# Two factor transfers swapped on ScalarE's queue, two merge groups regrouped by batch, and six fewer products of zeros, at the start of a conditioned mixture-of-experts kernel

## The reference, cut to what matters

```
def cond(x, ids, wi, wo, common, experts):      # first block, once per batch
    hidden = x @ wi.T + 2 * (x @ cia.T) @ cib.T + 2 * (x @ Eia[id].T) @ Eib[id].T
    hidden = relu(hidden)
    return hidden @ wo.T + 2 * (hidden @ coa.T) @ cob.T + 2 * (hidden @ Eoa[id].T) @ Eob[id].T
...
for r in range(4):                              # mixture of experts, on the result
    w = top-2 softmax of cur @ Wg[r] + bg[r]
    cur = cur + sum_e w_e * (gelu(cur @ W1[e] + b1[e]) @ W2[e] + b2[e])
x = x + cur
...                                             # second block: language factors, ternary net
```

## Time and profile before

| what | value |
|---|---|
| time before, median of 3 runs | 481.5 us (481.15 to 481.94) |
| the profiled execution's own time | 481.59 us |
| its span, first to last instruction | 479.9 us |
| TensorE busy | 475.6 us, 99% of the span |
| VectorE, ScalarE, GpSimd busy | 388.1, 393.7, 121.4 us |

### The profile page before, as it was taken

One profiled execution on the slowest core, in us unless ns is written; L12 is line 12 of the kernel. 1 busy time (PEld: TensorE's weight loads), 2 busy tenths in 40 slices (PEclk: granted clock), 3 DMA queues, 4 the chain that ended last, 5 costly groups with the idle time before them and its releaser, 6 DMA issues.

```text
span 479.9 us, 7453 instructions
## 1 busy us (share of the span) xinstructions
PE 475.6 (99%) x2268; PEld 396.2 (83%) x2268; DVE 388.1 (81%) x638; ACT 393.7 (82%) x543; POOL 121.4 (25%) x102
## 2 busy tenths in 40 slices
PE   9999999999999999999999999999999999999997
PEld 8998888888888888888888888888888888888886
DVE  4899899999989898988898898889897758654343
ACT  4889888888888898888888788898888888697644
POOL 3995212121211212121212121271313144500000
PEclk9999999999999999999999999999999999999999
DMA  7504702020120202020202012120202000000001
GB/s 237 188 24 133 286 1 89 2 88 13 77 82 6 88 0 88 0 88 0 88 1 87 23 65 84 48 89 0 88 2 88 2 0 0 1 1 0 0 23 69
DMA packets 8299, 27.03 MB, mean 56 GB/s; under 512 B 2258, under 2 KB 3602, under 8 KB 6098
## 3 DMA queue, kind: packets, MB, share of 16 engines
q1 hardware_dynamic: 7090, 22.45, 13.1%
q0 software_dynamic: 288, 2.88, 1.6%
q10 hardware_dynamic: 896, 1.38, 0.9%
HBM read 25.26 MB, written 1.44 MB: 56 GB/s over the span
## 4 chain that ended last, share of the span: by engine, by line
PE 97%; POOL 2%; DVE 0%; ACT 0%; issue 0%; DVEq 0%; POOLq 0%
PE bank L538 34%; PE bank L541 34%; PE bank L544 26%; POOL ffn_lo L442 1%; PE bank L634 1%; PE bank L638 1%; PE bank L639 1%; PE bank L565 1%; POOL xlo L447 0%; PE bank L562 0%; DVE stage L1076 0%; DVE prod L1076 0%; ACT ffn_hi L842 0%; DVE x L1312 0%; POOL blank L430 0%
## 5 line engine op out<-in xcount | busy, mean ns | idle before, releaser
L859 ACT ACTIVATE act_out<-bank,vec 128x512 f32<-128x512 f32 x256 | 165.0, 682 | 40.4 <-PE bank L544 28.2
L1154 DVE TENSOR_TENSOR hid_lo<-act_out,hid_hi 128x1024 fp32r<-128x1024 f32 x128 | 158.6, 1258 | 31.6 <-ACT hid_hi L864 31.5
L864 ACT ACTIVATE hid_hi<-act_out 128x1024 fp32r<-128x1024 f32 x128 | 135.9, 1062 | 8.2 <-ACT act_out L859 0.4
L502 POOL TENSOR_TENSOR cur<-cur,prod 128x512 f32<-128x512 f32 x48 | 64.9, 1352 | 233.6 <-DVE prod L1165 233.1
L538 PE MATMUL bank<-hid_hi,moe_hi 128*128 128x512 f32 x256 | 99.8, 390 | 0.0
L544 PE MATMUL bank<-hid_hi,moe_lo 128*128 128x512 f32 x256 | 99.7, 390 | 0.0
L541 PE MATMUL bank<-hid_lo,moe_hi 128*128 128x512 f32 x256 | 99.7, 389 | 0.0
L538 PE MATMUL bank<-xhi,moe_hi 128*128 128x512 f32 x256 | 99.6, 389 | 0.0
L541 PE MATMUL bank<-xlo,moe_hi 128*128 128x512 f32 x256 | 99.6, 389 | 0.0
L544 PE MATMUL bank<-xhi,moe_lo 128*128 128x512 f32 x256 | 99.6, 389 | 0.0
L538 PEld LDWEIGHTS bank<-hid_hi,moe_hi 128*128 128x128 f32 x256 | 48.1, 188 | 11.1
(11 more groups left out here) (134 smaller groups left out, 573.7 us busy)
## 6 DMA issues: line engine op xcount, KB each, us to landing
cw_all<-cw_dram SPq DMA_DIRECT2D x16, 1024.0 KB, 4.7
stage<-ffn_w POOLq DMA_DIRECT2D x1, 2304.0 KB, 8.5
cw_all<-moe_w SPq DMA_DIRECT2D x4, 512.0 KB, 6.9
stage<-lora_all SPq DMA_DIRECT2D x5, 160.0 KB, 3.8
x<-x_t SPq DMA_DIRECT2D x3, 256.0 KB, 4.2
out_t<-x SPq DMA_DIRECT2D x3, 256.0 KB, 2.5
cur<-cond_base ACTq DMA_DIRECT2D x2, 256.0 KB, 3.4
stage<-ffn_w POOLq DMA_DIRECT2D x1, 512.0 KB, 4.1
```

Source lines behind the costliest of these rows:

```text
L502: pool.tensor_tensor(cur[:, c, :], cur[:, c, :], prod[:, s % 2, :], ALU.add).then_inc(add_done, 1)
L859: act.activation(act_out[:, f // 2, f % 2, :], bank[:, f, :], ACT.Gelu_apprx_tanh, bias=vec[:, V_B1 + e * FC + f:V_B1 + e * FC + f + 1]).t ...
L864: act.activation(hid_hi[:, s % 2, 2 * pr:2 * pr + 2, :], act_out[:, pr, :, :], ACT.Copy)\
L1154: dve.tensor_tensor(hid_lo[:, s % 2, 2 * pr:2 * pr + 2, :], act_out[:, pr, :, :], hid_hi[:, s % 2, 2 * pr:2 * pr + 2, :].bitcast(F32), ALU ...
```

## The change

Three edits. In ScalarE's queue the second part of the base weights is issued ahead of the factors of batch 3 (the fourth batch). The third and fourth merge group, which held kind 0 and then kind 1 of batches 2 and 3, now hold both kinds of batch 2 and then both of batch 3, with banks 4 and 5 for batch 2 and 6 and 7 for batch 3. The products of zeros become ten (were 12) ahead of the first group and two (were 6) behind the second.

```
-                ((2, 0), (3, 0)),
-                ((2, 1), (3, 1)),
+                ((2, 0), (2, 1)),
+                ((3, 0), (3, 1)),
...
-MERGE_BANKS = (6, 7, 2, 3, 5, 4, 6, 7, 4, 6, 7, 4, 6, 7, 4, 6)
+MERGE_BANKS = (6, 7, 2, 3, 4, 5, 6, 7, 4, 6, 7, 4, 6, 7, 4, 6)
...
-WARM, KEEP_WARM = 12, 6
+WARM, KEEP_WARM = 10, 2
...
             first_load(act, 1)
+            base_load(act, 1)
             lora_load(act, 3)
-            base_load(act, 1)
```

## The result

The changed kernel takes 482.11 us (median of 22 executions, 481.50 to 485.75), the kernel before in the same session 481.51 us (22 executions, 480.52 to 482.24). The ratio is 1.0020, 95% interval 1.0011 to 1.0028. The forecast was 481.1 us, 0.4 us faster, in a range of 480.4 to 482.0. The changed kernel is slower by 0.6 us, just above the upper end of that range.

The account below looks back on a forecast made before the run. TensorE, busy 99%, bounds the kernel; only its start before 18.95 us can move. GpSimd's path gains 0.42 us and TensorE's 0.43, so 0.42 us off the 481.5 median gives 481.1 us, range 480.4 to 482.0.

Parts of the forecast that it names:

- What sets the time: Work from 18.95 us on moves as a block; the change is worth how much earlier that work starts.
- Ten leading products of zeros: TensorE's start: first group at 5.65 us, VectorE's first sum 0.42 us earlier, bounds 0 and 0.83 us.
- The third group: TensorE's merges: needs batch 2 alone, landing at 8.1 us, so it starts about 8.15 us.
- The swap: ScalarE's queue: batch 3's factors land at 8.5 us; second sum releases the fourth group at 8.85; swap alone worth nothing.
- late fourth batch: Fourth group: batch 3's factors queue behind 256 KB and slip; 481.4 to 481.5 us; chance 0.24 shared with similar cases.
- met even without the swap: VectorE's sum of (0, 1): second base part lands at 8.5 us, before the sum's start at 8.67.
- Regrouping at nothing: Third and fourth groups: strips run side by side, fourth takes at most 1.10 us; regrouping alone worth nothing.
- Two products of zeros behind the second group: TensorE free at about 8.1 us; removed 0.96 us is open on its side, other things then decide.
- The clock rival: TensorE at 1.2 GHz after pauses until about 14 us: 2.3 us lost, 483.4 us, +0.4%; chance 0.06.

Follow-up runs that it names:

- filled-in zeros: The changed kernel with four more products of zeros between the third and fourth merge group: 482.65 us against 481.33, ratio 1.0030.
- the old groups and a pause of 1.7 us: The kernel before with the swap and ten and two products of zeros, old merge groups kept: 482.15 us against 481.33, ratio 1.0022.
- zeros alone: The kernel before with ten and two products of zeros instead of twelve and six, transfers and groups as before: 480.90 us against 481.31, ratio 0.9993.

## Why the prediction was wrong

**What sets the time: right.** The work behind 19 us moved as a block (457.84 of 457.85 us busy after), and over the table the profiled time is 463.8 to 464.4 us more than the sixth group's start in all rows but that of eight leading zeros.

**Ten leading products of zeros: right in kind.** The first group starts at 5.66 us (forecast 5.65), set by the factors' landing. The first sum came 0.82 us earlier in the first trace and 0.23 in the second (7.66), around the forecast 0.42; but the kernel before has it at 7.46 in its second profile. TensorE's change of level comes at another time in each execution: the 24 passes of zeros took 5.49 us in one trace of the kernel before and 5.23 in the other. Alone, this edit measured 0.5 and 0.1 us faster, both within chance.

**The third group: right.** 7.97 us against 8.15, and 8.78 in the second trace, where batch 2's factors landed at 8.7.

**The swap: the step that failed.** The text took 8.5 us for the landing of batch 3's factors, "bounds 7.9 ... and 8.8", because ScalarE's two transfers together had landed by 8.5 before. They land at 9.1 to 9.5 us in the traces of five of the kernels above that have the swap, and at 8.8 only in the one with filled-in zeros. The sum of bytes on the queue did not hold: the transfer took 4.4 to 5.0 us from its issue where the bound allowed 4.2. Nor was the 3.3 us of the earlier trace rows firm: with the old order the same transfer takes 2.9 to 4.4 us in the ten traces and lands at 6.9 to 8.4, in the kernel's own second profile at 8.4. The fourth group was therefore released by a DMA at 9.54 and not by the second sum at 8.85, and first_hidden starts at 10.63 instead of 9.95. The rival "late fourth batch" named this mechanism but priced it as the loss of the gain, 481.4 to 481.5 us. It is more: in an execution with the landing at 9.4, first_hidden can't start before 9.54 + 1.09 = 10.63 us, while the kernel before reaches 9.96 in its second profile. That fits the fastest executions: 480.52 us before, 481.50 after; over all runs none of the kernels with the swap has an execution below 481.24, and those with the old order and the old groups all have some at 480.5 to 480.9, but for the one with eight leading zeros. So the swap takes away the early executions, as far as lowest times and single traces can tell. The text had one profile, at a late clock change, and measured the change against that one; the swap alone cost 0.67 us. With all products of zeros and the new groups the swap costs nothing that can be seen (ratio 1.0007 with it, 1.0008 and 1.0012 without), since the fourth group starts only at 9.2 to 9.3 us there anyway. What the swap bought is the second part of the base 1.1 us earlier (3.55 + 3.9 = 7.5 us). The text said that the third sum is "met even without the swap", and that is wrong for an early start: six of the ten traces without the swap show VectorE waiting for it. But the wait sets the time in two of them only.

**Regrouping at nothing: wrong, though hidden here.** The text let the products of both groups run side by side. The rows show that the fourth group's first product starts 0.56 us behind the third's although its factors, bank and strip are free, and first_hidden 1.65 us behind the third group's start instead of 1.10. The medians of the regrouping alone are 0.4 and 0.6 us above the kernel before, about as much as one kernel differs from itself here, so the loss of time is not shown by them.

**Two products of zeros behind the second group: right about the median, wrong about the tail.** The text took pauses of 0.2 us as harmless and expected none above 0.3 from 9 us on. The trace has one of 0.41, the wait for late factors, and in 7 of 34 executions of the changed kernel the mean granted clock is 0.993 to 0.996. None of these seven was traced, so that their clock falls behind that pause is argued from the runs with longer, shorter and filled pauses. With the old groups and a pause of 1.7 us it is 5 of 12, and one of these was traced. The clock rival was priced at a low clock until 14 us and 2.3 us lost; that trace shows the low clock until 13.2 us and 1.7 us lost. Its chance of 0.06 was near for the median and too low for single executions. The Trainium skill (TensorE: Matmul & The Clock Gate, "What's actually happening") says that the engine's default state is throttled and activity releases it; these traces agree, at 0.50 of the full clock behind the pause.

**What stays open.** Why the same bytes on one queue end later when the larger transfer goes first (at 8.8 to 9.5 us, against 8.3 to 8.8 in eight of the ten traces with the old order) was not tested. SyncE's queue is slower too in the pair of first profiles (batch 4's factors take 5.0 us from their issue at 5.83, against 4.2 from 5.96 before), but the second profile of the kernel before has 4.5, so this doesn't explain it. What makes the kernel with eight leading zeros 3 us slower is open as well. Nor is any version shown to beat the kernel before: the two best, zeros alone (0.9993, 0.9981 to 1.0006) and leading zeros alone (0.9993, 0.9984 to 1.0002, then 0.9996, 0.9987 to 1.0005), have intervals that hold 1.

## What to carry to other kernels

When a transfer is put ahead of another on busy queues, cost the second one by more than the issue that it lost: here 0.5 us of issue became 1 to 2 us of landing against most traces of the old order, and the work behind it had 0.1 us to spare by the forecast. A profile is one execution; where its start depends on a clock that rises at another time in each, take several profiles and compare lowest and median times as well, since a new wait can take away the early executions and leave the profiled one as it was. Before products that only keep TensorE busy are removed, find what it will wait for next, and look at single executions: the price may stand in every fifth one.

## What the runs showed that was not expected

- Products on different 32-row strips did not run freely side by side: the first product of the next group started 0.56 us behind the last group's 512-column product, just behind its second pass, in both traces of the regrouping alone.
- Between eight and ten leading products of zeros, with two behind the second group, lies a step of 3 us (484.45 against 480.90 us), while between ten and twelve there is none above chance. In the one trace of it the 1.7 us lost lie behind the last sum.
- Behind a pause of 1.7 us, which ended at 9.60, TensorE's granted clock fell to 0.50 and was full again only at about 13.2 us, although the engine was busy 2.00 of 2.00 us in each stretch from 10 us.
- The kernel before measured against itself came out at 1.0006 (0.9996 to 1.0016) with medians 0.47 us apart.
